# Other slots in a three-stage attention kernel, and one mask fewer on TensorE

## The reference

```
L0:  q, k, v = grouped conv (kernel 3, 8 heads of depth 16) of x, ctx, ctx   # 8 heads, 256 x 256 scores
     x = layernorm(softmax(q k / sqrt(8) - 1e9 mask) v + x) * gamma + beta
L1:  out1 = layernorm(x + mha(x, x, x, look_ahead_mask))        # 16 heads of depth 16
     out2 = layernorm(out1 + mha(ctx, ctx, out1, padding_mask)) # 16 heads, 128 x 128 scores
     out  = layernorm(out2 + relu(out2 w1 + b1) w2 + b2)
```

## Time and profile before

| what | value |
|---|---|
| median of 3 runs | 4481.46 us (4481.1 to 4481.8) |
| profiled execution, its own time | 4476.52 us |
| its span | 4474.7 us |
| TensorE busy (PE) | 4144.4 us, 93% |
| VectorE busy (DVE) | 3523.3 us, 79% |
| ScalarE busy (ACT) | 3136.7 us, 70% |
| GpSimd busy (POOL) | 2872.4 us, 64% |
| mean granted TensorE clock | 0.985 |

### The profile page before, as it was taken

The page is one execution under the profiler, slowest core; times in us unless marked ns, Lnnn a source line. Parts: engine busy times, 40 slices in busy tenths (PEclk is TensorE's granted clock), DMA queues, the critical chain, the costliest instruction groups (busy, mean ns, idle before and its releaser), DMA issues. The chain is left out here.

```text
span 4474.7 us, 129562 instructions
## 1 busy us (share of the span) xinstructions
PE 4144.4 (93%) x46216; PEld 3376.6 (75%) x46216; DVE 3523.3 (79%) x13839; ACT 3136.7 (70%) x6279; POOL 2872.4 (64%) x4568
## 2 busy tenths in 40 slices
PE   7999999999999969999999986999999997999999
PEld 5777777777777747777777765788787776999998
DVE  7898988989988859999999985777777774555555
ACT  5777777777777748888888875777777775444443
POOL 4777777777776637777777764766766762444444
PEclk9999999999999979999999998999999998999999
DMA  5444444444444436767777756898889882222221
GB/s 137 119 125 119 123 123 120 125 120 122 122 121 123 114 94 154 169 160 172 162 165 170 162 131 144 195 197 193 194 197 193 194 184 90 71 71 71 71 71 53
DMA packets 1082953, 608.79 MB, mean 136 GB/s; under 512 B 64664, under 2 KB 1082056, under 8 KB 1082312
## 3 DMA queue, kind: packets, MB, share of 16 engines
q1 hardware_dynamic: 1071896, 595.70, 54.8%
q10 hardware_dynamic: 10416, 4.80, 0.5%
HBM read 175.66 MB, written 117.54 MB: 66 GB/s over the span
## 5 line engine op out<-in xcount | busy, mean ns | idle before, releaser
L1142 DVE CUSTOM_DVE_ANT_0 l_junk<-l_bank,mask 128x256 bf16<-128x256 f32 x2048 | 776.8, 418 | 47.6 <-PE l_bank L830 33.7
L995 ACT ACTIVATE mha_probs<-mha_bank 128x512 f32<-128x512 f32 x1024 | 611.3, 601 | 278.9 <-DVE mha_bank L1157 154.0
L995 ACT ACTIVATE l_probs<-l_bank 128x512 f32<-128x512 f32 x1024 | 604.6, 597 | 266.2 <-DVE l_bank L1157 258.8
L1157 DVE TENSOR_TENSOR l_bank<-l_bank,mask0t 128x512 f32<-128x512 f32 x768 | 530.5, 691 | 25.9 <-PE l_bank L862 22.4
L1142 DVE CUSTOM_DVE_ANT_0 mha_junk<-mha_bank,mask 128x128 bf16<-128x128 f32 x2048 | 462.3, 284 | 29.7 <-PE mha_bank L830 29.4
L830 PE MATMUL l_bank<-l_stack 96*128 96x256 bf16 x2048 | 385.2, 274 | 58.8 <-DMA l_stack<-l_parts 29.6
L830 PE MATMUL mha_bank<-mha_stack 96*128 96x128 bf16 (+1 forms) x4096 | 355.8, 221 | 79.2 <-DVE mha_max_parts L1142 48.0
L1557 ACT ACTIVATE ffn_hidden<-ffn_h,ffn_b_s 128x512 f32<-128x512 f32 x256 | 176.4, 689 | 354.8 <-PE ffn_h L1504 344.1
L862 PE MATMUL l_bank<-l_stack 99*128 99x128 bf16 x4096 | 403.1, 221 | 9.7 <-ACT l_probs L995 4.3
L1157 DVE TENSOR_TENSOR mha_bank<-mha_bank,mask1t 128x512 f32<-128x512 f32 x512 | 354.9, 693 | 71.2 <-PE mha_bank L862 66.1
L862 PE MATMUL mha_bank<-mha_stack 99*128 99x128 bf16 (+1 forms) x4096 | 395.8, 220 | 15.4 <-DMA mha_stack<-mha_max_rows 13.6
(11 more groups left out here) (197 smaller groups left out, 11430.0 us busy)
## 6 DMA issues: line engine op xcount, KB each, us to landing
mha_stack<-mha_parts SPq DMA_DIRECT2D x1536, 128.0 KB, 3.5
l_stack<-l_parts SPq DMA_DIRECT2D x1024, 64.0 KB
l_stack<-l_parts SPq DMA_DIRECT2D x256, 128.0 KB
rows_o<-mha_resid SPq DMA_DIRECT2D x64, 512.0 KB, 3.5
cols_o<-mha_y_t SPq DMA_DIRECT2D x128, 256.0 KB, 3.0
l_x_pad<-in_x SPq DMA_DIRECT2D x64, 256.0 KB, 3.3
l_c_pad<-in_ctx SPq DMA_DIRECT2D x64, 256.0 KB, 3.2
l_resid<-in_x_t SPq DMA_DIRECT2D x64, 256.0 KB, 3.2
```

Source lines behind the costliest of these rows:

```text
L995: nc.scalar.activation(probs[:, i % RING, :], tbank[i % 2][:, :], ACT.Exp).then_inc(att_exp, 1)
L1142: ins = nc.vector.tensor_tensor_reduce(out=junk[:, i % 2, cols], in0=sbank[i % 2][:, cols], in1=mask, scale=1.0, scalar=LOWEST, op0=ALU.ad ...
L1157: nc.vector.tensor_tensor(bank_, bank_, mask.unsqueeze(1).to_broadcast([P, 4, P]), ALU.add).then_inc(att_masked, 1)
```

## The change

Only the table changes. In the first stage attention tile 15 is masked by VectorE instead of TensorE, seven of the 16 score chunks go to later slots, the first values step is no longer cut in two, and two turns of y come a slot earlier. In the second stage two score chunks and half of a values step move. In the third stage nine score chunks move to later slots and two to an earlier one, the turn of the heads comes one slot later, the turn of the maxima moves from slot 3 to 5 (second half) and from 9 to 12 (first half of the next unit), and projections, values and a turn of y are in other slots.

```diff
 first stage
-        score=[2, 3, 4, 6, 7, 8, 10, 10, 11, 12, 12, 13, 14, 14, 15, 16],
+        score=[3, 4, 5, 7, 7, 8, 10, 10, 11, 12, 12, 13, 14, 15, 16, 18],
-        pe_masks=(4, 12, 14, 15),
+        pe_masks=(4, 12, 14),
-        pool_steps={'add': (7, 0), 'power': (8, 1)},
-        work=[((0, 1), 'values', 1, 0),
+        pool_steps={'add': (7, 1), 'power': (8, 1)},
+        work=[((0,), 'values', 1, 0),
-              ((9,), 'turn_y', -1, 3),
+              ((8,), 'turn_y', -1, 3),
-              ((13,), 'turn_y', 0, 0),
+              ((12,), 'turn_y', 0, 0),
 second stage
-        score=[4, 4, 6, 8, 8, 9, 11, 12, 12, 13, 13, 14, 15, 15, 17, 18],
+        score=[4, 4, 7, 8, 9, 9, 11, 12, 12, 13, 13, 14, 15, 15, 17, 18],
-        pool_steps={'power': (9, 0)},
+        pool_steps={'power': (9, 2)},
-              ((5, 6), 'values', 1, 1),
+              ((5,), 'values', 1, 1),
 third stage
-        score=[2, 2, 4, 4, 6, 6, 8, 8, 11, 11, 12, 13, 13, 14, 15, 16],
+        score=[4, 4, 5, 7, 8, 8, 9, 9, 10, 10, 12, 13, 13, 14, 15, 18],
-        steps={'turn': 5, 'turn_merged': 7, 'output': 8, 'normalise': 9},
-        dve_steps={'recip': (5, 1), 'merge': (5, 2), 'low': (7, 1), 'add': (8, 1), 'stats': (8, 1), 'moments': (9, 0), 'epsilon': (9, 1)},
+        steps={'turn': 6, 'turn_merged': 7, 'output': 8, 'normalise': 9},
+        dve_steps={'recip': (5, 1), 'merge': (5, 1), 'low': (6, 2), 'add': (8, 2), 'stats': (8, 2), 'moments': (9, 1), 'epsilon': (9, 1)},
-              ((1,), 'values', 1, 1),
-              ((3,), 'max', 0, 1),
-              ((3, 4), 'project', 2, 0),
+              ((2,), 'values', 1, 1),
+              ((3,), 'project', 2, 0),
+              ((5,), 'max', 0, 1),
-              ((7,), 'turn_y', -1, 3),
+              ((9,), 'turn_y', -1, 3),
-              ((9,), 'max', 1, 0),
-              ((11,), 'project', 2, 3),
+              ((12,), 'max', 1, 0),
+              ((11, 12), 'project', 2, 3),
-        split_slot=14,
+        split_slot=13,
```

More of the change, by code:

```diff
@@ L97 @@
     dict(
-        score=[2, 2, 4, 4, 6, 6, 8, 8, 11, 11, 12, 13, 13, 14, 15, 16],
+        score=[4, 4, 5, 7, 8, 8, 9, 9, 10, 10, 12, 13, 13, 14, 15, 18],
         pv_lag=1,
-        steps={'turn': 5, 'turn_merged': 7, 'output': 8, 'normalise': 9},
-        dve_steps={'recip': (5, 1), 'merge': (5, 2), 'low': (7, 1), 'add': (8, 1), 'stats': (8, 1), 'moments': (9, 0), 'epsilon': (9, 1)},
+        steps={'turn': 6, 'turn_merged': 7, 'output': 8, 'normalise': 9},
+        dve_steps={'recip': (5, 1), 'merge': (5, 1), 'low': (6, 2), 'add': (8, 2), 'stats': (8, 2), 'moments': (9, 1), 'epsilon': (9, 1)},
         pe_masks=(),
         split_lag=0,
-        pool_steps={'power': (9, 2)},
+        pool_steps={'power': (9, 1)},
         work=[((0,), 'values', 1, 0),
-              ((1,), 'values', 1, 1),
-              ((3,), 'max', 0, 1),
-              ((3, 4), 'project', 2, 0),
+              ((2,), 'values', 1, 1),
+              ((3,), 'project', 2, 0),
+              ((5,), 'max', 0, 1),
               ((6,), 'turn_y', -1, 2),
               ((7,), 'project', 2, 1),
-              ((7,), 'turn_y', -1, 3),
+              ((9,), 'turn_y', -1, 3),
               ((9,), 'project', 2, 2),
-              ((9,), 'max', 1, 0),
-              ((11,), 'project', 2, 3),
+              ((12,), 'max', 1, 0),
+              ((11, 12), 'project', 2, 3),
               ((15,), 'turn_y', 0, 0),
               ((15,), 'turn_y', 0, 1)],
-        split_slot=14,
+        split_slot=13,
     ),
```

## The result

The changed kernel takes 4560.16 us (median of 4 runs, 4558.46 to 4568.73), the kernel before 4481.63 us (4481.1 to 4482.28): a ratio of 1.0179 (estimated from all the runs, as every ratio below; the medians alone give 1.0175), 95% interval 1.0161 to 1.0197. The forecast was 4540 us, range 4475 to 4605. The profiled execution took 4561.43 us, its span 4559.5 against 4474.7; the mean granted clock fell from 0.985 to 0.974.

What follows compares the result with a forecast made beforehand. TensorE's order and waits were taken to set the time. First stage -18, second -1, third +80 give +61 on 4476.5, that is 4538, with the median's 5 us 4542, said as 4540; range 4475 to 4605.

Steps and rivals of the forecast that it cites:

- The sign and the place: Slower by over 0.2% (0.77), through a wait in front of third-stage tile 8 for the maxima's rows; third stage +80 us.
- The stall's size: Third stage: rows need 6.6 us from turn to tile 8, TensorE has 3.2 us of work, so 3.4 us wait per unit.
- The returns: Third stage, per unit: 0.5 us back at the turn of heads, 0.3 from halving the maxima's wait; z's wait stays.
- The clock: Third stage: granted clock stays at 1.00; its fall was left to rival 3.
- the forecast's own 4515 to 4565: Whole kernel: the range of the forecast itself, apart from its rivals, chance 0.46.
- rival 3: Third stage: the stall halves the clock, costing +25 to +50 us more, 4570 to 4595 us; chance 0.20.
- The first stage: -18 us (-40 to +20): fills' wait of 22 us goes; removed mask becomes about 0.7 us wait at L913.
- Rival 4: First stage: VectorE becomes the bound with 0.6 us more per unit, +20 instead of -18, 4580 us; chance 0.12.
- The second stage: Two scores a slot later and an unsplit values step: -1 us, between -6 and +8.
- The rule: Engines serve queues packet by packet, so ScalarE's small DMA need not wait behind SyncE's backlog; third stage would lose nothing.
- rivals 1 and 2: Third stage: small DMA lands about 2.2 us after issue, 4447 us (0.10), or about 3.5 us, 4460 to 4485 (0.12).
- rival 2: Third stage: landing of about 3.5 us makes its net near zero, 4460 to 4485 us; chance 0.12.

Runs made afterwards that it cites:

- s3_rows_early: Changed kernel, but in the third stage the last score chunk back in slot 0 and the second half's maxima turn back in slot 3: 4468.84 us, 0.9975.
- s1_only: Kernel before with only the first stage's entry of the changed table: 4455.97 us, 0.9944.
- half_fills: Changed kernel, but SyncE issues only 6 of the 12 fills of each half in the third stage: 4453.79 us, 0.9943.
- half_fills_early: s1_only with only 6 of the 12 fills of each half in the third stage: 4445.03 us, 0.9927.
- mask_alone: Kernel before with first-stage attention tile 15 masked by VectorE instead of TensorE, no slot moved: 4475.01 us, 0.9995.
- slots_alone: s1_only with first-stage attention tile 15 still masked by TensorE, so the new slots without the moved mask: 4463.33 us, 0.9966.

## Why the forecast held and where it was off

**The sign and the place** were right. The stall in front of tile 8 is there, the two edits that make it late make the loss (`s3_rows_early`), and where it is short the changed third stage costs nothing against `s1_only` (`half_fills`), or some 7 us against `half_fills_early`, with the changed second stage in them.

**The stall's size.** Forecast 3.4 us, measured 2.7. L839 to issue took 0.77 (1.1 taken), issue to tile 5.3 (5.5 taken), the work between 3.4 (3054.11 to 3057.50, where the wait in front of tile 8 begins; 3.2 counted). 0.77 + 5.27 - 3.39 is the 2.65 of that unit.

**The returns.** 0.8 us per unit were taken, 0.5 for L887 and 0.3 for half of the maxima's wait. In `half_fills` the mean unit of 30.45 us holds 0.55 us of stall, so the rest of it is 29.9 against 30.5 in the kernel before: 0.6 came back. L887's part did, 0.5. The wait for maxima did not halve (20.6 us in `half_fills`, 19.1 in the changed kernel, 19.3 before), and the one for z at L913 gave 0.1.

**The clock** is the term that the forecast had wrong. It said 1.00 through the third stage and gave the fall of the clock 0.20 as a rival in place of its own number. It came on top: 1.35 us per unit, 43 us, inside that rival's +25 to +50. (On 4540 these give 4565 to 4590, not the 4570 to 4595 written there.) The sum with measured terms is 2.7 - 0.6 + 1.35 = 3.45 us per unit for 3.3 measured, times 31 +107 for +101. The row to trust was the earlier trace rows, a stretch as idle as the coming stall. Two errors cancelled in part, 0.7 us per unit too much stall and 1.35 too little clock; the 20 us between 4540 and 4560 are what is left. So it is luck in part that 4560 lies in the forecast's own 4515 to 4565: by the sign that the prediction itself named, a clock of 1.00 or else rival 3, rival 3 is what happened, on a shorter stall.

**The first stage.** Forecast -18, measured -25 (`s1_only`). The fills' wait went as said (22 us counted), and the mask was worth next to nothing as said (`mask_alone`, `slots_alone`). The mechanism for that was half right: TensorE does wait for z at L913, 0.15 us and not 0.7, because a wait of 0.65 for ScalarE's copy of the heads now stands one slot ahead at L887. That wait I had not seen. And with the old slots it is the maxima at L830 that take the mask's time back. Rival 4, VectorE as the bound, is out: the stage got faster with 13 masks per unit.

**The second stage.** Forecast -1, within -6 and +8; alone it is +1 and inside the error, in company perhaps +5.

**The rule and rivals 1 and 2** (a landing at once, or in 3.5 us) are out for this kernel, with issue to tile at 5.3 us. `half_fills` shows that rival 2's mechanism would have been right with half the fills: its landing is 3.1 us, its unit in the third stage equal to the one before, and its time, 4454 us, 6 under that rival's range.

## What to carry to other kernels

Before moving a step that ends in a small DMA, count the work of the waiting engine between issue and use, and set against it the time from issue to use of the same DMA under the same traffic, not a free DMA's: here 5.3 us with the fills, 3.3 with half of them. When a new stall of TensorE comes out at 2 us or more, price the clock with it; in this kernel it was half again of the stall, 1.35 us on 2.7. And removing work from the bounding engine is worth what is left after the next wait behind it: 0.55 us of mask gave 0.1.

## What the hardware showed that I had not expected

- The clock's price rises steeply with the stall: at 2.7 us per unit 17 of 99 groups of products ran slow, at 1.7 us 7 of 104, at 1.3 us 1 of 101. Of 46 stalls under 1.5 us none was followed by half clock, of 38 between 2 and 3 us 30 were, of 14 longer ones all. Matmuls whose result is overwritten, laid into the stall, made the kernel 43 us faster.
- The completion of a 24 KB DMA went from 5.5 to 2.5 us with half the fills of another issuing queue, where 209 KB instead of 537 KB of them were waiting. In the same kernel, at the same busy share of 0.59, another such DMA took 4.6 us, with 666 KB waiting.
- Waits trade places nearly one for one: 15 us less of TensorE's busy time in `mask_alone` became 15 us more wait for VectorE.
